# Channel attention in a twelve-stage decoder kernel: scores issued interleaved, numerator and denominator in one product, result turned, root of the norm on GpSimd

## The reference

```python
def _L3_xattn_ref(q, k, v, gamma):      # (16, 128, 256) each
    qh = q.reshape(B, 8, 16, 256)       # 8 heads of 16 rows
    kh = k.reshape(B, 8, 16, 256)
    vh = v.reshape(B, 8, 16, 256)
    qk = einsum('bhdq,bhdl->bhql', qh, kh) / 4
    sm = softmax(qk, axis=-1)           # 256 x 256 per head
    ret = einsum('bhql,bhdl->bhdq', sm, vh)
    return gamma * ret.reshape(B, 128, 256)
x = layernorm(x + _L3_xattn_ref(x, ctx_2048, ctx_2048, gamma))
```

## Time and profile before

| | us |
|---|---|
| median of three runs | 3990.88 |
| lowest and highest | 3988.33, 3993.56 |
| the profiled execution's own time | 3998.22 |
| its span | 3996.4 |

### The profile page before, as it was taken

How to read it: one execution, slowest core, us unless ns; L and a number is a source line. 1 busy time by engine, 2 the same in 40 slices (tenths; PEclk the granted TensorE clock), 3 DMA queues, 4 the chain that set the end, 5 groups by cost and what they waited for, 6 DMA issues and landing times. The chain is left out here.

```text
span 3996.4 us, 65697 instructions
## 1 busy us (share of the span) xinstructions
PE 3464.1 (87%) x23619; PEld 2190.9 (55%) x23634; DVE 3056.8 (76%) x6556; ACT 1946.2 (49%) x4750; POOL 1167.3 (29%) x1208
## 2 busy tenths in 40 slices
PE   7799999999884485879899979889999999997875
PEld 3466666665553243654566655565655556564544
DVE  6799989989657766562477858869888888885678
ACT  4466666666553142421244434436655556563445
POOL 1533033306302100000011222106655555563210
PEclk9899999999997698989999989899999999997887
DMA  2222222222211100001000000311212222121000
GB/s 69 62 73 57 66 63 67 50 73 56 52 40 32 35 1 24 2 1 62 23 1 1 1 33 2 121 40 69 82 64 74 69 74 74 69 75 61 2 1 22
DMA packets 240529, 184.36 MB, mean 46 GB/s; under 512 B 117776, under 2 KB 216720, under 8 KB 239312
## 3 DMA queue, kind: packets, MB, share of 16 engines
q1 hardware_dynamic: 240208, 180.16, 15.0%
HBM read 164.88 MB, written 15.20 MB: 45 GB/s over the span
## 5 line engine op out<-in xcount | busy, mean ns | idle before, releaser
L310 PE MATMUL ps<-xT,min 128*128 128x512 f32 (+1 forms) x1072 | 505.1, 616 | 31.1 <-DVE macc L3358 30.8
L3358 DVE SCALAR_TENSOR_TENSOR macc<-ps,mcw,macc 128x508 f32<-128x508 f32 (+2 forms) x408 | 302.4, 741 | 82.7 <-ACT macc L3285 72.8
L3440 POOL TENSOR_TENSOR mSQ<-mSQ,mtn 128x512 f32<-128x512 f32 x128 | 239.9, 1874 | 365.7 <-ACT mtn L3310 365.6
L310 PEld LDWEIGHTS ps<-xT,min 128*128 128x128 f32 (+1 forms) x1072 | 192.3, 191 | 251.5 <-issue 204.8
L3433 POOL TENSOR_TENSOR mE<-mE,mCB 128x1024 f32<-128x1024 f32 x128 | 302.4, 2362 | 44.5 <-DVE mE L3368 26.5
L3368 DVE TENSOR_TENSOR_SCAN mE<-mE,mid 128x1024 f32<-128x1024 f32 x128 | 297.1, 2321 | 0.0
L3218 PE MATMUL ps<-mwo,macc 128*128 128x256 f32 x1024 | 245.0, 382 | 5.4 <-DVE macc L3375 5.4
L2946 ACT ACTIVATE hE<-ps 128x512 f32<-128x512 f32 x256 | 139.0, 595 | 220.9 <-PE ps L2908 220.9
L3306 ACT ACTIVATE mtn<-ps,mcol 128x64 f32<-128x64 f32 x1024 | 222.9, 334 | 3.0 <-PE ps L3197 2.8
L826 POOL TENSOR_TENSOR dTB<-did,dNB 128x1024 f32<-128x1024 f32 (+1 forms) x10 | 28.6, 2864 | 667.7 <-DMA dNB<-d_N 603.5
L2976 DVE TENSOR_REDUCE hMX<-ps 128x2 f32<-128x512 f32 x256 | 158.9, 684 | 60.0 <-PE ps L2887 60.0
(11 more groups left out here) (589 smaller groups left out, 8448.3 us busy)
## 6 DMA issues: line engine op xcount, KB each, us to landing
mE<-m_decay SPq DMA_DIRECT2D x128, 512.0 KB, 3.6
dwk<-in_L_attn_Wk SPq DMA_DIRECT2D x64, 128.0 KB, 2.3
dwq<-in_L_attn_Wq SPq DMA_DIRECT2D x64, 128.0 KB, 2.4
dwv<-in_L_attn_Wv SPq DMA_DIRECT2D x64, 128.0 KB, 2.4
dwg<-in_L_attn_Wg SPq DMA_DIRECT2D x64, 128.0 KB, 2.4
dwo<-in_L_attn_Wo SPq DMA_DIRECT2D x64, 128.0 KB, 2.7
min<-in_m_in SPq DMA_DIRECT2D x2, 4096.0 KB, 17.8
d_N<-dNT SPq DMA_DIRECT2D x256, 16.0 KB, 1.5
```

The lines of the kernel that those rows point to most:

```text
L310: t = pe.matmul(out, w[:, j, :], self.c.xT[:, j, blk(g, 512)], start=j == 0, stop=j == 1)
L3358: x = dve.scalar_tensor_tensor(out=acc[:, :, 3 - j:T], in0=p[:, :, 0:T - 3 + j], scalar=self.cw[:, i, j:j + 1], in1=acc[:, :, 3 - j:T], op ...
L3440: pool.tensor_tensor(self.SQ[g % 2][:, :], self.SQ[g % 2][:, :], self.tn[s][:, :], ALU.add).then_inc(*self.sqa.up)
```

## The change

Stages 8 and 11 are reordered and partly rewritten.

- The four `t` steps and the two `s` steps of one iteration become four steps `scores` (k = 0 to 3). Each holds eight products: four turned ones of block t-2 on two row groups and four plain ones of block t on the other two, issued in turns. Each kind has three banks (0 to 2 plain, 3 to 5 turned) that it goes round, and every maximum and every exponential now sends its own signal.
- The numerators and the denominators come from one set of 16 products: the stationary `VE` holds 16 columns of values and 16 columns of ones for every head. ScalarE writes its values straight from PSUM; VectorE has filled the tiles with ones at the stage's start. GpSimd's masked copies and the tile `P1` go.
- The result stands with channels on the columns and is turned: ScalarE copies bank 6, TensorE turns it in four transposes (`ot`), VectorE takes the reciprocal of 16 columns and multiplies, TensorE turns the quotient back in two transposes (`back`), VectorE adds x.
- The statistics are taken block by block (`stat`); aggregation and scaling of a group of four (`norm_step`) stand between the maxima of later blocks; the root is an addition and a power on GpSimd (`norm_pool`). In the last steps they are issued one behind the other.
- One iteration works on five blocks, so there are 20 of them, where there were 19; `XE` and `KE` have four sets. The side step of the next stage stands at the end of an iteration.

```diff
     def buffers(self):
...
-        self.KE, self.XE, self.VE, self.V, self.MX, self.E, self.O = (c.sets(n, "h" + m, *z) for n, m, *z in (
-            (3, "KE", 2, D), (3, "XE", 2, D), (3, "VE", 2, 2, 128), (2, "V", 2, 128), (2, "MX", 2, 128), (2, "E", 8, 2, D), (2, "O", 2, D)))
-        self.R, self.P1 = [c.R, c.f32("hR", 4, D)], c.f32("hone", 2, 128)
+        self.KE, self.XE, self.VE, self.MX, self.E, self.O, self.Y, self.rd = (c.sets(n, "h" + m, *z) for n, m, *z in (
+            (4, "KE", 2, D), (4, "XE", 2, D), (2, "VE", 2, 4, 2, 32), (2, "MX", 2, 128), (2, "E", 8, 2, D), (2, "O", 512), (2, "Y", D), (2, "rd", 16)))
...
     def order(self):
...
+        yield "keys", 0, 0
+        for t in range(NB + 4):
+            for step, b, k in (("keys", t + 1, 0), ("stat", t - 5, 0), ("t", t - 2, 0), ("s", t, 0), ("sh", t - 1, 0), ("vt", t - 2, 0),
+                               ("t", t - 2, 1), ("s", t, 1), ("o", t - 3, 0), ("t", t - 2, 2), ("s", t, 2), ("ot", t - 3, 0),
+                               ("t", t - 2, 3), ("s", t, 3), ("back", t - 4, 0)):
+                if step == "s" and t < NB + 2:
+                    yield "scores", t, k
                 if 0 <= b < NB:
                     yield step, b, k
...
+            if t in self.ASIDE:
+                yield "aside", *self.ASIDE[t]
+            if t == NB:
+                yield "norm", 2, 0
+        yield "stat", NB - 1, 0
+        yield "norm", 3, 0
+    def norm_step(self, dve, own, g, k):
+        c = self.c
+        if k == 0:
+            dve.wait_ge(own.sem, self.last)
+            if g:
+                dve.wait_ge(*self.rq.at(g))
+            for j in range(4):
+                x = dve.bn_aggr(c.st[:, j, 6:8], c.st[:, j, 0:6])
+            x.then_inc(*self.var.up)
+        else:
+            dve.wait_ge(*self.rq.at(g + 1))
+            c.scale_vector(dve, g, self.R[g % 2])
+    def norm_pool(self, pool, own, g):
+        c = self.c
+        pool.wait_ge(*self.var.at(g + 1))
+        o = own(pool.tensor_scalar(self.pw[:, 0:4], c.st[:, :, 7:8].rearrange("p a b -> p (a b)"), 1e-5, 1.0, ALU.add, ALU.mult))
+        pool.wait_ge(own.sem, o)
+        pool.tensor_tensor(c.rsq[:, 0:4], self.pw[:, 0:4], self.pw[:, 4:8], ALU.pow).then_inc(*self.rq.up)
+    def scores(self, pe, t, k):
+        room, b, x = self.c.room, t - 2, (t - 2) % 4
+        e, rr = divmod(k, 2)
+        turned, plain = 0 <= b, t < NB
+        tb, sb = ([(8 * n + 2 * k + i) % 3 + z for i in range(2)] for n, z in ((b, 3), (t, 0)))
+        if turned:
+            if k == 0:
+                pe.wait_ge(*self.xs.at(b + 1))
+            for n in tb:
+                pe.wait_ge(*room[n])
+        if plain:
+            if k == 0:
+                pe.wait_ge(*self.xe.at(t + 1))
+                pe.wait_ge(*self.ke.at(t + 1))
+            for n in sb:
+                pe.wait_ge(*room[n])
+        for h in range(2):
+            if turned:
+                for i, n in enumerate(tb):
+                    r = blk(2 * rr + i, 32)
+                    m = pe.matmul(self.c.bank(n)[:, blk(h, 256)], self.KE[x][r, e, blk(h)], self.XE[x][r, e, :], start=True, stop=True)
+                if h:
+                    m.then_inc(*self.tr.up)
+            if plain:
+                for i, n in enumerate(sb):
+                    r = blk(2 * (1 - rr) + i, 32)
+                    m = pe.matmul(self.c.bank(n)[:, blk(1 - h, 256)], self.XE[t % 4][r, h, blk(e)], self.KE[t % 4][r, h, :], start=True, stop=True)
+                if h:
+                    m.then_inc(*self.sc.up)
+        for i in range(2):
+            if turned:
+                room[tb[i]] = self.ex.at(8 * b + 2 * k + i + 1)
+            if plain:
+                room[sb[i]] = self.mx.at(8 * t + 2 * k + i + 1)
...
+            elif step == "scores":
+                self.scores(pe, b, k)
...
             elif step == "o":
...
+                pe.wait_ge(*room[6])
...
+                for e in range(2):
                     for lt in range(2):
                         for r in range(4):
...
+                            t = pe.matmul(bank(6)[blk(r, 32), blk(e, 256)], self.VE[y][:, lt, r, e, :], self.E[y][:, 2 * r + e, lt, :],
+                                          start=lt == 0, stop=lt == 1)
+                t.then_inc(*self.o.up)
+                room[6] = self.oc.at(b + 1)
+            elif step == "ot":
+                pe.wait_ge(*room[6])
+                for n in range(4):
+                    t = pe.transpose(bank(6)[:, blk(n)], self.O[y][:, blk(n)], c.ident[:, :])
+                t.then_inc(*self.ot.up)
+                room[6] = self.mul.at(b + 1)
+            elif step == "back":
+                pe.wait_ge(*room[7])
+                pe.wait_ge(*self.mul.at(b + 1))
+                for qt in range(2):
+                    t = pe.transpose(bank(7)[:, blk(qt)], self.Y[y][:, blk(qt)], c.ident[:, :])
+                t.then_inc(*self.bk.up)
+                room[7] = self.sum.at(b + 1)
...
+                    act.wait_ge(*self.o.at(b - 1))
+                act.copy(self.VE[y][:, :, :, :, 0:16].rearrange("p l r e c -> p (l r) e c"),
+                         bank(6)[:, 0:256].rearrange("p (w e c) -> p w e c", e=2, c=16)).then_inc(*self.ve.up)
             elif step == "t":
...
+                    n = (8 * b + 2 * k + i) % 3 + 3
+                    act.activation(self.E[y][:, 2 * (2 * rr + i) + e, :, :], bank(n).rearrange("p (n q) -> p n q", n=2), ACT.Exp,
+                                   scale=0.25).then_inc(*self.ex.up)
...
     def vector(self, dve, own):
         c, bank = self.c, self.c.bank
...
+        dve.wait_ge(*self.prev.ended())
...
+            o = dve.memset(self.VE[y][:, :, :, :, :].rearrange("p l r e c -> p (l r e c)"), 1.0)
+        o.then_inc(*self.row1.up)
         dve.wait_ge(own.sem, r)
...
             if step == "s":
...
+                for i in range(2):
+                    n, r = (8 * b + 2 * k + i) % 3, 32 * (2 * (1 - k % 2) + i)
+                    dve.tensor_reduce(self.MX[y][:, k // 2, r:r + 32:16], bank(n).rearrange("p (e n) -> p e n", e=2), AX.X, ALU.max,
+                                      negate=True).then_inc(*self.mx.up)
+                    late, w = (b - 8) % 4, 2 * k + i - 1
+                    if b >= 8 and w >= 0 and 7 * late + w in (0, 12):
+                        self.norm_step(dve, own, (b - 8) // 4, 7 * late + w)
+            elif step == "stat":
+                dve.wait_ge(*self.sum.at(b + 1))
+                self.last = own(dve.bn_stats(c.st[:, j, 0:6], self.R[g % 2][:, j, :]))
...
+            elif step == "ot":
+                dve.wait_ge(*self.ot.at(b + 1))
+                p = bank(6).rearrange("p (e w h c) -> p e w h c", e=2, h=2, c=16)
+                rd = self.rd[y][:, :].rearrange("p (e w) -> p e w", e=2)
+                if b >= 2:
+                    dve.wait_ge(*self.bk.at(b - 1))
+                r = own(dve.reciprocal(rd, p[:, :, :, 1, 0]))
                 dve.wait_ge(own.sem, r)
+                dve.tensor_tensor(self.Y[y][:, :].rearrange("p (w e c) -> p e w c", e=2, c=16), p[:, :, :, 0, :],
+                                  rd.unsqueeze(3).broadcast_to([128, 2, 8, 16]), ALU.mult).then_inc(*self.mul.up)
+            elif step == "back":
+                R = self.R[g % 2][:, j, :]
+                dve.wait_ge(*self.bk.at(b + 1))
                 if self.GAMMA:
...
+                    a = dve.scalar_tensor_tensor(out=R, in0=bank(7)[:, 0:256], scalar=self.gm[:, 0:1], in1=c.X[:, b, :], op0=ALU.mult, op1=ALU.add)
...
+            elif step == "norm":
+                for n in (0, 12):
+                    self.norm_step(dve, own, b, n)
...
+            if step == "norm":
+                self.norm_pool(pool, own, b)
+            elif step == "s" and k == 1 and b >= 8 and b % 4 == 0:
+                self.norm_pool(pool, own, b // 4 - 2)
+            elif step == "keys":
...
                 for e in range(2):
                     i = pool.tensor_scalar(self.XE[x][:, e, :], c.X[:, b, :], self.par[:, e:e + 1], 1.0, ALU.mult, ALU.mult)
                 i.then_inc(*self.xe.up)
                 for e in range(2):
                     i = pool.tensor_scalar(self.KE[x][:, e, :], self.ctx[:, b, :], self.par[:, e:e + 1], self.row[:, e:e + 1], ALU.mult, ALU.add)
                 i.then_inc(*self.ke.up)
...
-                if b >= 3:
-                    pool.wait_ge(*self.o.at(b - 2))
-                for e in range(2):
-                    i = pool.tensor_tensor(self.VE[x][:, :, e, :], self.V[b % 2][:, :, :], bc(self.rp[:, e, :], 2), ALU.mult)
-                i.then_inc(*self.ve.up)
```

More of the change, by code:

```diff
@@ L2834, in buffers @@
         c = self.c
[L2835 to L2837 removed]
+        self.KE, self.XE, self.VE, self.MX, self.E, self.O, self.Y, self.rd = (c.sets(n, "h" + m, *z) for n, m, *z in (
+            (4, "KE", 2, D), (4, "XE", 2, D), (2, "VE", 2, 4, 2, 32), (2, "MX", 2, 128), (2, "E", 8, 2, D), (2, "O", 512), (2, "Y", D), (2, "rd", 16)))
```

(40 more changed lines are left out.)

96 lines of the change are left out of this document (21 added, 75 removed).

## The result

| | us |
|---|---|
| before, median (lowest to highest) | 3989.61 (3981.69 to 3993.56) |
| after, median (lowest to highest) | 3934.92 (3928.34 to 3940.05) |
| after / before | 0.9856, 95% interval 0.9842 to 0.987 |
| forecast, range | 3923, 3890 to 3968 |
| profiled execution after: its own time, span | 3935.08, 3933.3 |

The change gives 55 us where 68 were forecast. The two profiled executions are 63.1 us apart: that of the kernel before is 8.6 above its median, that of the kernel after is at it. The first stage went from 207.0 us to 183.7 (2335.42 to 2519.13), the second from 236.2 to 206.4 (3613.13 to 3819.49): 53.1 us in the places that the change touches.

A forecast was written before the change was run, and what follows sets the result against it. TensorE's own work bound the two stages' blocks (10.76 us); afterwards VectorE's order would. First stage 31 and second 37 us less, 68 in sum, take the median from 3990.9 to 3923, range 3890 to 3968.

The forecast's parts named there:

- TensorE's work per block: One steady block at full clock: TensorE's work falls by 2.95 us to 7.81.
- the third rival: Score steps: the two kinds of products do not overlap, a step costs 1.93 rather than 1.06; 4006 us, chance 0.02.
- The period: Steady block: the longest loop, set by VectorE's order, takes 8.87 us; 9.2 in the mean with scalings.
- "one more" wait: Steady block: VectorE waiting again for scores that could not start, 1.22 us more, excluded by margins of 0.05 and 0.14.
- VectorE's order: Steady block: the sequence of VectorE's steps, not TensorE's 7.81, sets the period of 8.87 us.
- first rival: Steady blocks: emptying PSUM holds more than the loop, 10.1 us per block; 3954 us, chance 0.20.
- The first stage: First channel-attention stage: 174.5 us against 207.0, with 3.2 left for falls of the clock; 31 us gained in all.
- The second stage: Second channel-attention stage: 201.2 us against 236.2, including 11 for side steps and 15.7 for low clock.
- The clock term: Second stage: half of the 31.5 us lost at the low clock before stays, 15.7, range 0 to 31.
- The root: Norm's root: two GpSimd instructions, 1.0 us together; only the last root of each stage is paid.
- The clock rival: Steady blocks: the chip answers TensorE's waits with the low clock, 13.9 us per block; 4045 us, chance 0.08.
- the fourth, all hidden: Both stages: side steps stay hidden and the clock holds throughout; 3893 us, chance 0.12.

The follow-up runs named there:

- d_back_early: Kernel after, with transposes back, residual sum and statistics of a block issued behind step 1's scores and maxima instead of at the block's end; 3936.34 us, ratio 0.988.
- h_fine: Kernel after, with each score step split into two halves that wait for their own banks and signal separately; 3902.47 us, ratio 0.9792.
- g_aside_mid: Kernel after, with the following stage's side steps back in the middle of a block instead of at its end; 3929.46 us, ratio 0.9851.
- j_fine_aside: Kernel after, with score steps split in halves and the next stage's side steps in the middle of a block; 3896.66 us, ratio 0.977.
- e_root_only: Kernel before, with only the norm's root moved to two GpSimd instructions; 3971.68 us, ratio 0.996.
- a_root_dve: Kernel after, with the norm's root back on VectorE as its twelve small instructions; 3951.32 us, ratio 0.9908.
- b_apart: Kernel after, with each score step issuing its four turned products first and its four plain ones behind them; 3943.55 us, ratio 0.9884.

## Why the prediction was right, and where it was 13 us off

**TensorE's work per block.** Forecast 7.81, read 7.92; scores 1.07 to 1.08 for 1.06, numerators 1.86, result transposes 0.66. Right, and with it the third rival (no overlap, 1.93 a step) is out.

**The period.** Forecast 8.87, read 9.15. The step that failed is the loop's end: "one more" wait was excluded because step 3's scores would be there 0.05 before VectorE asks. They came 0.15 late. I had priced a first maximum and its way to TensorE at 0.62 + 0.08 = 0.70; it is 0.84 (0.68 for one maximum from start to end, 0.16 to the next product). The 0.14 counts once at the loop's end and once, as 0.15 of wait, ahead of step 3's maxima: that is the 0.28. With it the loop is another one: not VectorE's order but three handoffs. By the forecast's own prices these were 3 x 1.92 + 2.92 = 8.68, just under the 8.87 of VectorE's order; by the measured ones they are 9.15. d_back_early and h_fine show which of the two held the block. My first rival named this mechanism and overpriced it at a whole 1.22. The Trainium skill, TensorEngine Tiling (Array Packing), PSUM Bottleneck, said that emptying may be the bound after tiling: the trace agrees, and makes it a delay of 2.07 per pair of banks, not a lack of VectorE time (7.27 busy of 9.15). 26 x 0.28 = 7 us.

**The first stage.** Forecast 177.7 (174.5 and 3.2 for the clock), read 183.7. The two first blocks took 23.7 for 22.7, the third 9.3 for 11.9, the thirteen steady ones 123.9 for 121.3 (the period's 3.6 more, 1.0 less for scalings and clock), the end 26.7 for 21.8. So most of the shortfall is in the last steps, where TensorE stood at the low clock (0.50 from 2502.2 to 2509.0) while VectorE ran a chain of the next stage's small instructions: from step 1 to step 2 it took 5.6 us (2502.97 to 2508.55) where the block before took 2.9, and the numerators 3.64 instead of 1.86.

**The second stage.** Forecast 201.2, read 206.4. Here the end took 27.3 for 21.8, the two first blocks 23.7 for 22.7 and the third 13.2 for 11.9, while the thirteen steady blocks took 142.2 for 144.8: their period was 3.6 too short in the forecast, and the 29.5 for scalings, side steps and clock were 6.3 too much. That the sum came out so near is luck. The clock term itself had no ground. I left 15.7 for low clock in the seven blocks where 31.5 were lost before; the same seven (shift 3688.48 to 3759.91) now take 71.4, 7.4 over seven periods, and the windows from 3690 to 3760 stand at 1.00 but for one of 0.86 and one of 0.97, so little of the 7.4 can be the clock; scalings and side steps stand in these blocks. Why the low stretches of before are gone stays open. It is not the side steps' new place: with them back in the middle (g_aside_mid) the windows stay at 0.89 and above from 3670 to 3770, and the new place costs some 9 us of stage 2 (g_aside_mid, j_fine_aside). In the execution of e_root_only, where only the root had moved, the seven blocks took 91.4 instead of 106.8, so half of that loss went with the root; it is one execution. The low clock at the start lasted longer than before, some 43 us from the first scores at 3613.13 against some 33 (3645.38 to about 3679).

**The root.** GpSimd's two instructions were taken as 1.0 and are 0.20 + 1.01, with 1.41 of wait for VectorE. The first stage's end chain is 3.67 for 5.65, 2.0 of the 2.5. The second's stayed at 5.69, since the four scalings there take 3.39 instead of 1.38. They now run beside an instruction of the next stage on GpSimd, which stands behind the last root in its stream and so starts when the root is done (VectorE and GpSimd, first the kernel before, then the kernel after):

```profile
3846.46 2.36 POOL L2593 TENSOR_TENSOR X<-X,qb 128x1024 f32<-128x1024 f32 x1
...
3885.86 1.38 DVE L246 TENSOR_SCALAR X<-hR,st,rsq 128x256 f32<-128x256 f32 x4
```
```profile
3821.72 2.34 POOL L2593 TENSOR_TENSOR X<-X,qb 128x1024 f32<-128x1024 f32 x1
3821.79 3.39 DVE L246 TENSOR_SCALAR X<-hR,st,rsq 128x256 f32<-128x256 f32 x4 [1.41 <-POOL rsq L2885]
```

The first of the four takes 2.42 us instead of 0.41 in every kernel that has the root on GpSimd, and 0.41 in a_root_dve, where GpSimd was through with it long before (3801.85). An engine that is given a step in another's chain also delays what stands behind that step, and here it brought it to the worst moment. Inside the stages the root's removal is worth more than I knew: 16 us in all.

**The sum.** The forecast was 68, the stages and ends give 55: 6.0 short in the first stage, 5.2 in the second, 3.0 at the two ends, less the 1.4 that I had set aside for filling the tiles, which the executions do not show.

**The clock rival.** It did not happen: the steady blocks have waits of TensorE and stand at 1.00. Nor did the fourth, all hidden: side steps, ends and the low clock at the starts all cost time.

## What to carry to other kernels

When a change takes work off the bounding engine, write down the loop through two engines and a buffer as well: here first product to first result, result to freed bank, freed bank to next product, times the steps per block. Where neither engine is busy for the whole period, look for that loop first; here it yielded to finer waits on the same work (32 us) and not to moving work (0). A side condition that holds by 0.05 us in such a sum should be priced as failed. And when a small step moves to another engine, look at what stands behind it there.

## What the runs showed of the hardware

- **VectorE's small instructions beside GpSimd.** In the kernel before, the same root instructions take 0.16 us until GpSimd begins at 2424.20, and then up to 0.74 (VectorE and GpSimd, kernel before):

```profile
2424.01 0.16 DVE L212 TENSOR_TENSOR rsq<-rsq 128x4 f32<-128x4 f32 x1
...
2424.20 1.41 POOL L3032 TENSOR_TENSOR hVE<-hV,hrp 128x256 f32<-128x256 f32 x2 [7.35 <-PE ps L2921]
2424.21 0.74 DVE L214 SCALAR_TENSOR_TENSOR rsq<-rsq 128x4 f32<-128x4 f32 x1
...
2424.98 0.65 DVE L210 SCALAR_TENSOR_TENSOR rsq<-rsq 128x4 f32<-128x4 f32 x1
```

  The chain took 4.4 us there. In a_root_dve it took 2.8: 0.19 to 0.35 for each instruction beside GpSimd's tensor_scalar work, 0.16 from its end on. The Trainium skill, SBUF — State Buffer, Who interferes with whom, has a VectorE instruction with two SBUF inputs contend with a GpSimd instruction that reads SBUF; the rows above have two, and the trace agrees. It does not cover all of it: three instructions with one SBUF input (L196, L205, L207) took 0.35, 0.20 and 0.27 beside GpSimd in a_root_dve, for 0.16 to 0.17 alone, and a scaling with one took 2.42 for 0.41 (above).
- **Products on different row groups overtake.** In b_apart plain products start 0.03 us behind the first turned one, ahead of turned ones issued before them (starts are the profile's records); a step takes 1.09 and a block 9.27, where the theory of a queue kept in order had 11.3.
- **The low clock at a stage's start ended sooner where TensorE had fewer gaps.** After: busy 5.0 to 8.0 of 10 us in the four windows at 0.50, some 43 us low in all. h_fine: 9.45 and 10.00 busy, at 1.00 from 3630 on, some 25 us low; part of that busy time is only the spread of a step's products over its two halves. That the gaps are the reason was not tested by itself.
- **GpSimd's power on 128x4 takes 1.01 to 1.05 us** and an addition of the same size 0.20.
